# Attention of a paged-cache decoder: from tiles of one kv head with four query heads to tiles of one query head of four kv heads

## The reference, cut to what matters

```
q = rope(rmsnorm(x Wq^T))    # 32 query heads of HD = 128
k = rope(rmsnorm(x Wk^T)); v = x Wv^T       # 8 kv heads of 128
kc, vc = k_cache[block_table], v_cache[block_table]   # 16 pages of 32 keys = 512
valid_c = arange(512) < cache_seqlens          # then 32 own keys, always valid
scores = q k_all^T / sqrt(128), -1e30 where not valid   # query head h uses kv head h // 4
o = softmax(scores) v_all
x = x + o Wo^T
```

## Time and profile before

| | |
|---|---|
| median of two runs | 2340.33 us (2339.3 to 2341.36) |
| span of the profiled execution | 2339.1 us |
| TensorE busy in the span | 2311.7 us, 99% |
| weight loads busy | 1999.4 us, 85% |
| VectorE, ScalarE, GpSimd busy | 1488.0, 1356.3, 508.3 us |
| moved by DMA | 488.63 MB |

### The profile page before, as it was taken

One profiled execution on the slowest core, in us unless ns is written; L12 is line 12 of the kernel. 1 busy time (PEld: TensorE's weight loads), 2 busy tenths in 40 slices (PEclk: granted clock), 3 DMA queues, 4 the chain that ended last, 5 costly groups with the idle time before them and its releaser, 6 DMA issues.

```text
span 2339.1 us, 48442 instructions
## 1 busy us (share of the span) xinstructions
PE 2311.7 (99%) x14320; PEld 1999.4 (85%) x14320; DVE 1488.0 (64%) x4154; ACT 1356.3 (58%) x4300; POOL 508.3 (22%) x538
## 2 busy tenths in 40 slices
PE   8999999998999999999999999999999999999998
PEld 7887777777999999999999999999998888888886
DVE  5899999983666666666666666666665344334433
ACT  4878888874666666666666666666665222222221
POOL 5211221211223333332222222222223011011101
PEclk9999999999999999999999999999999999999998
DMA  5344444448999999898998999999885333333331
GB/s 207 92 126 114 112 127 116 111 113 283 342 344 293 294 290 289 292 290 289 294 289 283 295 295 292 289 290 295 292 295 178 99 101 106 93 100 108 94 101 43
DMA packets 400360, 488.63 MB, mean 209 GB/s; under 512 B 63136, under 2 KB 334752, under 8 KB 397216
## 3 DMA queue, kind: packets, MB, share of 16 engines
q1 hardware_dynamic: 363296, 351.93, 49.3%
q0 software_dynamic: 36864, 134.23, 17.2%
HBM read 397.89 MB, written 88.08 MB: 208 GB/s over the span
## 4 chain that ended last, share of the span: by engine, by line
PE 77%; DVE 15%; issue 4%; SPq 1%; DMA 1%; DVEq 1%; ACT 0%; ACTq 0%
PE s_bank L1010 20%; PE o_bank L1022 19%; PE pt L1057 10%; DVE q_t L668 5%; PE proj L1509 5%; PE proj L1511 5%; PE proj L1510 5%; DVE part_s L659 5%; DVE q_t L684 5%; PE o_bank L1038 2%; PE slim L1540 1%; PE wide L1556 1%; PE wide L1551 1%; PE wide L1552 1%; PE turn L1530 1%
## 5 line engine op out<-in xcount | busy, mean ns | idle before, releaser
L977 DVE CUSTOM_DVE_ANT_0 probs<-s_bank,mask 128x544 f32<-128x544 f32 x512 | 371.1, 725 | 426.5 <-PE s_bank L1010 425.0
L931 ACT ACTIVATE probs<-probs,neg_max 128x544 f32<-128x544 f32 x512 | 383.9, 750 | 405.1 <-DVE neg_max L977 405.1
L1010 PE MATMUL s_bank<-k_t,q_t 128*128 128x288 f32 (+1 forms) x2048 | 558.3, 396 | 6.6 <-DMA q_t<-q_spill 4.4
L1022 PEld LDWEIGHTS o_bank<-p_t,v_c 128*128 128x128 f32 x4096 | 527.9, 192 | 28.8
L1022 PE MATMUL o_bank<-p_t,v_c 128*128 128x128 f32 x4096 | 540.1, 275 | 0.0
L1010 PEld LDWEIGHTS s_bank<-k_t,q_t 128*128 128x128 f32 x2048 | 351.2, 192 | 63.4 <-DMA q_t<-q_spill 4.8
L138 POOL DMA_INDIRECT v_c<-in_v_rows,v_row x256 | 255.2, 997 | 300.9 <-PE o_bank L1022 260.3
L1057 PE MATMUL pt<-ident,probs 128*128 128x128 f32 x2048 | 311.3, 275 | 0.0
L737 PE MATMUL acc<-w_hi,x_hi 128*128 128x512 f32 x764 | 304.6, 399 | 0.1
L903 ACT ACTIVATE p_t<-pt 128x512 f32<-128x512 f32 x512 | 295.9, 578 | 10.3 <-PE pt L1057 1.2
L738 PE MATMUL acc<-w_lo,x_hi 128*128 128x512 f32 x764 | 299.8, 392 | 0.0
(11 more groups left out here) (152 smaller groups left out, 3299.8 us busy)
## 6 DMA issues: line engine op xcount, KB each, us to landing
k_t<-in_k_pages SPq DMA_DIRECT2D x1024, 128.0 KB
q_spill<-wo_early SPq DMA_DIRECT2D x512, 64.0 KB, 1.8
q_t<-q_spill SPq DMA_DIRECT2D x64, 512.0 KB
o_spill<-o_t SPq DMA_DIRECT2D x64, 512.0 KB, 5.3
raw<-o_spill SPq DMA_DIRECT2D x64, 512.0 KB, 3.5
k_t<-in_w_qkv SPq DMA_DIRECT2D x11, 1024.0 KB, 5.7
v_spill<-wo_early SPq DMA_DIRECT2D x8, 1024.0 KB, 6.6
k_spill<-wo_early SPq DMA_DIRECT2D x128, 64.0 KB, 1.8
```

Source lines behind the costliest of these rows:

```text
L931: nc.scalar.activation(probs[:, j % SLOTS_P], probs[:, j % SLOTS_P], ACT.Exp, scale=-1.0, bias=neg_max[:, j % 2:j % 2 + 1], accum_out=row_ ...
L977: nc.vector.tensor_tensor_reduce(out=probs[:, j % SLOTS_P], in0=s_run, in1=mask[:, par], scale=-SCALE, scalar=3.0e38, op0=ALU.add, op1=ALU ...
L1010: last = pe.matmul(s_bank[:, columns].rearrange("p (s t) -> p s t", t=PSIZE), q_t[:, par, g], k_t[:, par, slots, g], start=True, stop=True)
L1022: last = pe.matmul(o_of(n), v_c[:, par, c, g * HD:(g + 1) * HD], p_t[:, i, c], start=g < QUAD and c == 0, stop=False)
```

## The change: what it does

A unit's tile is now one query head of four kv heads (g = 2a + hh for a = 0..3) times 32 tokens. Its 128 rows come from four matmuls of 32 weight columns each, on the four column groups of the array, and each streams the keys of its own kv head; there are two column ranges, so eight matmuls a unit. The scores have two buffers instead of one.

ScalarE multiplies the weights by the inverted sum, all 544 columns, in place of VectorE. VectorE turns the weights in 32x32 blocks into `p_t`, in place of TensorE, and there is nothing more to copy from PSUM for it. The values are weighed once for four units: 17 slots (16 pages and the own keys) times four matmuls of 32 rows of contraction, 128 weight columns and 128 moving columns, on the four row groups and into four banks. The work goes by periods of two units: on TensorE two scores and then half of a `weigh_values`, three periods behind.

In DRAM a page now holds its keys and its values side by side, 2 KB in each of 128 rows, and one DMA loads both; the indirect gather is gone. There are three page buffers. Of Wo 8 heads are split during attention instead of 20. In `project` buffers change places, and the first two batches' pages are asked for before their own keys.

```diff
-SLOTS = NPP + 2
+SLOTS = NPP + 1
+BUFS = 3
+VALUES = HK * PSIZE
+PAGE = VALUES + 2 * HD
-HI_EARLY = 20
+HI_EARLY = 8
...
+                    sp.dma_start(kv[:, buf_of(b), i],
+                                 kv_pages[bass.ds(page[i], 1)].rearrange("b d n -> (b d) n")).then_inc(pages_in[buf_of(b)], 16)
...
# SyncE in attend
+            for b in range(B):
+                if b >= BUFS:
+                    sp.wait_ge(summed, 4 * (b - BUFS + 1))
+                if b >= 2:
+                    load_pages(sp, b)
+                    load_own_keys(sp, b)
+                load_v_own(b)
+                if b >= 2:
+                    sp.wait_ge(scored, (b - 1) * HK)
+                    load_queries(sp, b)
+                if b in WO_WITH:
+                    h = WO_WITH[b]
+                    sp.dma_start(wo_early[:, h:h + HS], wo_t[:, h:h + HS, :]).then_inc(wo_in, 16)
+                if b >= BUFS:
+                    store(b - BUFS)
...
# ScalarE
+            def normalise(n):
+                i = n % SLOTS_P
+                act.wait_ge(inverted, n + 1)
+                nc.scalar.activation(probs[:, i], probs[:, i], ACT.Copy, scale=inv_sum[:, i:i + 1]).then_inc(normed, 1)
...
+            for t in range(PERIODS):
+                done = t - SUM_LAG
+                if done > 0 and done % 4 == 0:
+                    evacuate(done // 4 - 1)
+                if t > 0:
+                    normalise(2 * t - 2)
+                    normalise(2 * t - 1)
+                weigh(2 * t)
+                weigh(2 * t + 1)
...
# VectorE
+            def turn(n):
+                m, r = n // REP, n % REP
+                dve.wait_ge(normed, n + 1)
+                if r == 0:
+                    at_least(dve, summed, 2 * (m - 1))
+                nc.vector.transpose(p_t[:, m % 2, :, r], probs[:, n % SLOTS_P].rearrange("p (c e) -> p c e", e=S))\
+                    .then_inc(turned, 1)
...
+            for t in range(PERIODS):
+                lower_scores(2 * t)
+                lower_scores(2 * t + 1)
+                if t >= 1:
+                    turn(2 * t - 2)
+                invert(2 * t)
+                if t >= 1:
+                    turn(2 * t - 1)
+                invert(2 * t + 1)
+                if t % 4 == 0 and t // 4 + 1 < B:
+                    build_mask(t // 4 + 1)
...
# TensorE, score
+                    pe.wait_ge(masked, n - 1)
                 for columns, slots in ((slice(BANK - CUT * PSIZE, BANK), slice(0, CUT)),
                                        (slice(BANK, BANK - CUT * PSIZE + KEYS), slice(CUT, NPP + 1))):
-                    last = pe.matmul(s_bank[:, columns].rearrange("p (s t) -> p s t", t=PSIZE), q_t[:, par, g],
-                                     k_t[:, par, slots, g], start=True, stop=True)
+                    for a in range(QUAD):
+                        g, rows = 2 * a + hh, slice(a * S, (a + 1) * S)
+                        last = pe.matmul(s_banks[n % 2][rows, columns].rearrange("p (s t) -> p s t", t=PSIZE),
+                                         q_t[:, b % 2, g, r * S:(r + 1) * S],
+                                         kv[:, buf, slots, g * PSIZE:(g + 1) * PSIZE], start=True, stop=True)
...
# TensorE, values
+                for c in range(CUT) if half == 0 else range(CUT, SLOTS):
                     for a in range(QUAD):
                         rows = slice(a * S, (a + 1) * S)
+                        if hh == 0 and c == 0:
+                            at_least(pe, o_out, (b - 1) * QUAD + a + 1)
+                        last = pe.matmul(o_banks[a][:, hh * ROWS:(hh + 1) * ROWS],
+                                         kv[rows, buf, c, VALUES + hh * HD:VALUES + (hh + 1) * HD],
+                                         p_t[rows, m % 2, c].rearrange("p r s -> p (r s)"),
+                                         start=hh == 0 and c == 0, stop=hh == 1 and c == SLOTS - 1)
+                last.then_inc(summed, 1)
+
+            for t in range(PERIODS + SUM_LAG):
+                if t < PERIODS:
+                    score(2 * t)
+                    score(2 * t + 1)
+                if t >= SUM_LAG:
+                    weigh_values(t - SUM_LAG)
```

More of the change, by code:

```diff
@@ L110, in decoder @@
             in_page_i = sb("in_page_i", [P, 1], I32)
             key_index = sb("key_index", [P, L])
[L112 to L120, removed]
+            tables = (seq_f, pages, in_page_i, key_index)
@@ L121, in load_keys, with load_pages @@
+            pages_in = [sem(f"pages_in{i}") for i in range(BUFS)]
+            q_in = [sem("q_in0"), sem("q_in1")]
+            def load_pages(sp, b):
                 _, page = nc.values_load_multi_w_load_instructions(
-                    pages[0:1, bass.ds(b * NPP, NPP)], engines=[mybir.EngineType.SP], min_val=0,
+                    pages[0:1, b * NPP:(b + 1) * NPP], engines=[mybir.EngineType.SP], min_val=0,
                     max_val=PAGES - 1, skip_runtime_bounds_check_because="the table names pages of the cache")
@@ L169, in decoder @@
             place[0] += 2 * CH * P * 4
-            assert place[0] <= v_start + KC * HK * HD * 4
+            up2, up2_lo = after("up2", [2 * LOWS, D], "up2_lo")
+            assert place[0] <= kv_start + 2 * BUF_BYTES
             early_bytes = place[0] - q_start
@@ L397, in _, with first_pages @@
                 sp.dma_start(x_raw[:, q % 2], x_t[q]).then_inc(x_in[q % 2], 16)
[L399 to L403, removed]
+            def first_pages(b):
+                if b == 0:
+                    sp.wait_ge(consts_in, 16 * 3)
                     sp.wait_ge(x_split, len(PIECES))
@@ L895, in _ @@
-            for p in range(1, PAIRS):
-                emit(p)
+            for h in range(HI_EARLY):
+                pool.wait_ge(normed, (SPLIT_FROM + h) * HK + 2)
+                upper_weights(h)
+                pool.wait_ge(normed, (SPLIT_FROM + h) * HK + 6)
+                lower_weights(h)
         @block.scalar
         def _(act):
-            def pt_evacuate(n, i):
-                act.wait_ge(turned, n + 1)
-                at_least(act, summed, n - 1)
-                nc.scalar.activation(p_t[:, i].rearrange("p c n -> p (c n)"), pt[i][:, :], ACT.Copy).then_inc(pt_out, 1)
@@ new lines, in _ @@
+            for t in range(PERIODS):
[7 more added lines that the diff above has]
+                weigh(2 * t + 1)
+            normalise(UNITS - 2)
+            normalise(UNITS - 1)
+            for c in range(2):
+                split_upper(act, 0, c)
+            evacuate(B - 1)
@@ L999, in _, with score @@
+            turn(UNITS - 2)
+            turn(UNITS - 1)
+            for c in range(2):
+                split_lower(dve, 0, c)
         @block.tensor
         def _(pe):
-            def score(n, p, j):
-                par, g = j // HK, j % HK
-                if g == 0:
-                    pe.wait_ge(qk_in[par], 16 * QK_DMAS * (p + 1))
-                at_least(pe, masked, n)
-                if n == 0:
-                    pe.wait_ge(copied, NV * NT - 4)
+            def score(n):
+                b, hh, r = n // HK, n % HK // REP, n % REP
+                buf = buf_of(b)
+                if n % HK == 0:
+                    pe.wait_ge(pages_in[buf], 16 * (NPP + 1) * (b // BUFS + 1))
+                    pe.wait_ge(q_in[b % 2], 16 * (b // 2 + 1))
+                if n < 2:
+                    pe.wait_ge(copied, NV * NT - 4 + 2 * n)
+                else:
+                    pe.wait_ge(masked, n - 1)
@@ L1036, in weigh_own @@
                     for a in range(QUAD):
                         rows = slice(a * S, (a + 1) * S)
-                        last = pe.matmul(o_of(q * QUAD + a), v_own[rows, b % 2, q], own_t[rows, q], start=False,
-                                         stop=q == QUADS - 1)
-                last.then_inc(own_summed, 1)
-            def turn_own(quad):
-                pe.wait_ge(pt_out, (quad * QUAD + OWN_AFTER - LAG - 1) + 1)
-                pe.transpose(pt[0][:, 0:ROWS], own_of(quad * QUAD), ident[:, :]).then_inc(own_turned, 1)
@@ L1047, in turn @@
-            def turn(n):
-                i = n % 2
-                at_least(pe, pt_out, n - 1)
-                if n == 0:
-                    pe.wait_ge(copied, NV * NT)
-                pe.wait_ge(normed, 2 * n + 2)
-                if n % QUAD == 0:
-                    at_least(pe, own_out, n // QUAD)
-                for c in range(KC):
-                    last = pe.transpose(pt[i][:, c * ROWS:(c + 1) * ROWS], probs[:, n % SLOTS_P, c * P:(c + 1) * P], ident[:, :])
-                last.then_inc(turned, 1)
@@ L1060, in emit @@
-            def emit(p, first):
-                for j in range(UNITS):
-                    n = p * UNITS + j
-                    score(n, p, j)
-                    if n >= OWN_AFTER and (n - OWN_AFTER) % QUAD == 0:
-                        turn_own((n - OWN_AFTER) // QUAD)
-                    if n >= LAG + 1:
-                        weigh_values(n - LAG - 1)
```

(4 more changed lines are left out.)

386 lines of the change are left out of this document (128 added, 258 removed).

## The result

The changed kernel takes 2231.6 us (2230.25 to 2232.94, two runs) against 2340.33: the ratio is 0.9535, 95% interval 0.9517 to 0.9553, so 109 us or 4.65% faster. Its profiled execution spans 2231.1 us. Four later runs of the same kernel, beside runs of the kernel before, gave 2227.8 to 2247.3 us, ratio 0.9548 (0.9521 to 0.9575). The kernel before stayed within 2337.3 and 2343.0 in all its runs: the new one spreads more, and part of this study is why.

A forecast was written before the change was run, and what follows sets the result against it. TensorE bound attention at 19.1 us a batch, with DMA near. At 16.8 a batch, 64 x 16.8 + 18 = 1093 us replaces 1224.6; with +2 for the last stage, 2211 us, likeliest 2160 to 2270, full range 2135 to 2450.

The forecast's parts named there:

- the likeliest case: Whole kernel: all four column groups overlap fully, 2160 to 2270 us; chance 0.58.
- Four column groups at once: Score matmuls on TensorE: four column groups stream together, so a unit's scores still cost 0.92 us.
- the rival: Scores on TensorE: column groups don't work at once; 3600 us if all take turns; chance 0.20 for all its forms.
- TensorE's sum of 16.4 us a batch: Attention on TensorE: scores 7.36, values 7.55 and switches 1.44 us make 16.4 (14.9 to 17.0) against 19.1.
- VectorE 14.2, ScalarE 12.7 to 13.5: Attention: predicted work per batch in us on these two engines, both below TensorE's 16.4.
- I take 16.8 us a batch: Attention's steady batch, chosen with TensorE at 16.4 and DMA at 16.0 to 17.4 us nearly equal.
- rival 2: Attention: partial column overlap, TensorE's feeding or DMA eats most of the gain; 2280 to 2380 us; chance 0.14.
- The third buffer gives the loads five periods of slack: Page loads in attention: neither TensorE nor DMA waits much for the other's irregularities; a period is 4.1 us.
- Switches as a cost to be saved: TensorE's changes to row groups and back: 4 x 0.36 = 1.44 us a batch (0 to 2).
- Rival 3: Attention: free change between tiled modes, 2 KB rows at 3.0 us/MB or better; 15.6 us a batch, 2135 us; chance 0.08.
- Outside the steady state: Pipeline start +5, end +3, Wo loads +10, last stage +2 us; projection stays at 550 us.

## Why the prediction was right, point by point

The predicted 2211 us missed by 21 of the 2231.6, inside the likeliest case's range (2160 to 2270).

- *Four column groups at once*: right, though no row of before showed it, so it was a bet on the row groups' behaviour, and it held: a unit's four slots take 0.93 us, where 0.92 was put. The run on one column group gave 3559 where the rival had 3600. The rule of the Trainium skill that I cited against the change, loads overlap only matmuls of another row group (TensorE: Matmul & The Clock Gate, Part 3), doesn't show here: four loads of 0.11 us hide beneath each slot. The 2.38 for three column tiles that the same section of the Trainium skill states is 0.79 of the full factor; the runs here, with other widths and in a long stream, give 3.8 of four, 0.95.
- *TensorE's sum of 16.4 us a batch*: 16.3 in every undisturbed batch. Values 68 x 0.111, as in the earlier trace rows; a pair of changes costs 0.31 to 0.32 us by the starts instead of 0.36.
- *VectorE 14.2, ScalarE 12.7 to 13.5*: 617.2 and 672.7 us over 52.35 batches are 11.8 and 12.9 us. VectorE's was too high because durations overlap at their ends; ScalarE's product took the upper end of its bounds, 0.750, and the sum left out the reading of its accumulator, 0.193 us a unit. Neither mattered.
- *"I take 16.8 us a batch"*: this is the term that was mis-sized. The steady part took 17.2, which is 25 us over 64 batches; the ends took some 3 us less than the 18 put for them, so attention took 1114.8 where 1093 was forecast, all of the miss. I looked for the excess in the transfer of pages, at 16.0 to 17.4. The runs show the engines able to move a batch in 16.3, at 336 GB/s, and put most of the excess into instruction packets behind the full engines. That the number came near is thus partly luck: 16.8 was about halfway between TensorE's sum and the upper end for DMA, and the excess had another cause. The cause was among rival 2's, the feeding of TensorE, with 48 records and loads per us as its warning. It came on top of TensorE's sum, not in its place.
- *"The third buffer gives the loads five periods of slack"*: the head start was right, the slack not. SyncE's 12.3 us and the landing of 5.8 use 18 of 20.4 us; 12 us were lost there in the stretch looked at, and with a head start of one period instead of five 950 us.
- *Switches as a cost to be saved*: not tested by the prediction, but the runs with fewer of them show that a term of the sum can't be taken back alone.
- *Rival 3's 15.6 us a batch*: it doesn't follow from its own premise. 5.5 MB at 3.0 us/MB are 16.5 us, above TensorE's 14.9. The shortest batch, 16.32 us, is TensorE's own.
- *Outside the steady state*: the last stage +2.4 against +2, projection -0.5 against 0. The start cost some 12 us over TensorE's rhythm in its first 60, of the 18 that I had for both ends and Wo.

## What to carry to other kernels

Small float32 tiles on the four row or column groups ran side by side here at nearly full speed, but they multiply TensorE's instructions, and these travel through the same DMA engines as the data. Where the engines are as full as here (0.96), count instructions per microsecond as a transfer of its own. Look where the gaps stand in the instruction stream: here a constant place modulo 256 named the cause, and the landings of the packets confirmed it. When an engine's time falls, recount the head start of every load from the event that releases its buffer to its landing, SyncE's issue time included, before changing the order on TensorE.

## What the runs showed of the hardware that I had not expected

- TensorE's instructions came in packets of 16 KB, 256 instructions each. In the changed kernel and in the run with the queries moved, all 35 + 53 gaps of 0.3 us or more in the middle of batches stood at one place modulo 256, and in the changed kernel each ended 1.2 to 1.6 us after a packet's landing. At 800 records and loads a batch they cost 29 us with a DMA share of 0.96 and 6 with 0.70; at 392 a batch nothing.
- The execution time spread at the same time: 2227.8 to 2247.3 us for the same kernel, where the kernel before stayed within 6 us. The traces of two of its executions, of 2233 and 2247 us, have 29 and 41 us of such gaps.
- Changing from the row groups to the column groups costs some 0.11 us going by the starts (0.22 instead of 0.11), and the way back 0.1 for the change and 0.1 more before the second group of values.
